# Where normalised tokens are transposed in a fused graph-network kernel: TensorE and PSUM, or VectorE blocks and DMAs

## The chip, the cores and the metric

The kernel runs on one core of a Trainium2 chip. The metric is the device time of one execution in microseconds (us), the median of several runs. Beside it stands a profiled execution, whose records (the trace) give each instruction's start and duration on TensorE, VectorE, ScalarE, GpSimd and SyncE, and each DMA's issue and landing.

## The reference

The input is x, 128 graphs of 64 nodes with 256 features, and an adjacency matrix for each graph. Two blocks are computed, each added to its input. The first is one graph-attention layer with 8 heads. The second is three layers of attention, layer norm and feed-forward network, and the change is in that one:

```
h = relu(layernorm(x))                       # input of the second block
for l in range(3):
    si, sj = x @ attn_w[l, :d], x @ attn_w[l, d:]
    scores = leaky(si[:, :, None] + sj[:, None, :] + attn_b[l])
    attn = softmax(where(mask, scores, -inf))
    agg  = einsum('bij,bjd->bid', attn, x)
    h    = layernorm(x + agg, g1[l], beta1[l])
    ff   = gelu(h @ W1[l] + b1[l]) @ W2[l] + b2[l]      # 256 -> 1024 -> 256
    x    = layernorm(h + ff, g2[l], beta2[l])
```

All is in float32. Products of the feed-forward network are made from rounded values and remainders: hi x hi, lo x hi and hi x lo.

## The kernel before

The program has two parts. The first (lines 112 to 561) runs the first block; the second (lines 563 to 1150) runs the three layers. In the second part the 8192 tokens lie in 64 tiles of 128 (two graphs each); four tiles make a group of 512 tokens, and there are 16 groups. A lap takes four groups (QG) through three layers, so 12 slots (SLOTS), and there are four laps: 48 slots. In a slot the feed-forward network of one unit U (a group in a layer) is computed, and the attention and norm of the next unit, U + 1, are prepared beside it. There is no scheduler: each engine has its own program, and the order in each function `some` is the order of the engine's instructions. Semaphores tie them: `wait_ge` on an engine, and `pause` on the queues.

What an engine does in a slot s, in order (c is one of the 8 chunks of 128 hidden features):

- TensorE: `hidden(c)`, six matmuls of 512 columns out of nT_hi and nT_lo (normalised tokens, features on partitions) into one of three PSUM banks; two chunks later `output(c)`, twelve matmuls of 256 columns out of hid_hi and hid_lo. Behind hidden(0) stands `turn_attn`, behind hidden(1) `aggregate`, behind output(0) `spread`, and behind output(3), in the step c = 5, `turn_n` of U + 1: eight transposes of 128x128 from n_tok to the two banks NT_B, which are AGG's too. `hidden(0)` waits until nT_lo is made (s_nlo).
- ScalarE: `gelu(c)` in place in PSUM, `high(c)` (hid_hi, rounded), in c = 2 and 3 `norm_y`, in c = 4 `norm_n` (n_tok of U + 1), in c = 5 `split_n` (nT_hi, rounded from NT_B), and at the end `exp` of U + 2, with a table load on either side.
- VectorE: `take_y` (feed-forward result plus base), `row_sums`, `stats_y`, `spread_y` for U - 1 and the next; `low(0)`, `low(1)` (hid_lo, the remainders); `residual` and `stats_n` of U + 1; `low(2)`, `spread_n`, `low(3)`, `scores` of U + 2, `low(4)`, `low(5)`, `split_n` (nT_lo), `low(6)`, half of `dots_of` of U + 3, `low(7)`, the other half, `diagonal`.
- GpSimd: `make_base` (n_tok times g1 plus c1, in place, for take_y), `scale_y`, `finish`, `scale_n`, `post`.
- SyncE: `exchange` of U + 2 (two DMAs that bring the other graph's half of x to x_other), `put_out` and `refill` in some slots (stores and loads of 512 KB).

The wait at the start of `hidden` and the two halves of the split read:

```
if c == 0:
    pe.wait_ge(s_nlo, KD * (U + 1))
...
act.wait_ge(s_nT, KD * V + k + 1)
act.copy(nT_hi[:, s % 2, k, :], NT_B[k][:]).then_inc(s_nhi, 1)
...
dve.tensor_tensor(nT_lo[:, s % 2, k, :], NT_B[k][:], nT_hi[:, s % 2, k, :].bitcast(F32),
                  ALU.subtract).then_inc(s_nlo, 1)
```

## Time and profile before

| | us |
|---|---|
| median of 3 runs | 1663.23 |
| lowest and highest | 1660.3, 1664.78 |
| profiled execution, its own time | 1663.78 |
| its span, first to last instruction | 1662.0 |
| TensorE busy | 1524.7 (92%) |
| VectorE busy | 1378.4 (83%) |
| ScalarE busy | 1087.1 (65%) |
| GpSimd busy | 891.4 (54%) |
| mean granted TensorE clock, share of full | 0.972 |

Busy time counts the instructions of an engine, not its waits. A busy TensorE isn't an engine at its peak, as matmuls are pipelined and overlap in the records; the distance from one start to the next tells more than a duration. The first hidden chunk of the second part starts at 385 us, so some 1275 of the 1662 us are slots. In the trace L12 is line 12 of the kernel, an arrow points from what is read to what is written, and a bracket names how long the engine had been idle and what released it. SPq is SyncE's queue; an entry there is the time that the issue of a DMA takes, not the transfer.

### The profile page before, as it was taken

The page shows a single profiled execution, that of the slowest core. Times are in us where ns is not written, and L with a number is a line of the kernel's source. Part 1 is how long each engine was busy: PE and PEld are TensorE (multiplying, and loading weights), DVE is VectorE, ACT ScalarE, POOL GpSimd, SP SyncE. Part 2 cuts the span into 40 slices and gives each one's busy share as a digit, 9 for nine tenths or more (in the row PEclk, how much of TensorE's full clock was granted, in tenths as well). Part 3 has the DMA queues.
Part 4 walks back from the last instruction along what each step waited for, and adds up shares of the span by engine and source line. Part 5 has one row for each costly group of instructions (what it writes and reads, how often), then busy time and mean ns, then how long its engine had stood idle before and what let it go on. Part 6 is the DMA issues. An engine that isn't in the chain of part 4 may idle for free. (4 is left out here: it accounts for less than half of the span.)

```text
span 1662.0 us, 37278 instructions
## 1 busy us (share of the span) xinstructions
PE 1524.7 (92%) x11360; PEld 1282.6 (77%) x11360; DVE 1378.4 (83%) x4302; ACT 1087.1 (65%) x1946; POOL 891.4 (54%) x1008
## 2 busy tenths in 40 slices
PE   6888888827999999998999999899999999999995
PEld 6566666616888888887888888788888888888885
DVE  2889999967988989887888988888898888988852
ACT  1667777714677677665767666576777766677663
POOL 1667777723455355563545456444545656355464
PEclk9999999957999999999999999999999999999998
DMA  6233333250000011110001111100011211000001
GB/s 183 81 122 120 100 113 113 77 186 18 7 14 14 13 39 47 57 62 11 7 14 29 45 49 64 34 8 14 14 39 29 80 33 39 7 14 7 14 26 51
DMA packets 70894, 83.00 MB, mean 50 GB/s; under 512 B 29264, under 2 KB 54096, under 8 KB 70736
## 3 DMA queue, kind: packets, MB, share of 16 engines
q1 hardware_dynamic: 69104, 74.76, 15.2%
q0 software_dynamic: 816, 3.15, 0.6%
q10 hardware_dynamic: 816, 3.15, 0.5%
q8 instruction: 80, 1.31, 0.3%
q14 instruction: 78, 0.64, 0.1%
HBM read 38.95 MB, written 25.17 MB: 39 GB/s over the span
## 5 line engine op out<-in xcount | busy, mean ns | idle before, releaser
L805 ACT ACTIVATE bank<-bank,b_col 128x512 f32<-128x512 f32 x384 | 253.0, 659 | 365.2 <-PE bank L753 364.9
L765 PE MATMUL bank<-w_hi,hid_hi 128*128 128x256 f32 x1536 | 443.3, 289 | 17.8 <-DVE hid_lo L965 13.0
L765 PE MATMUL bank<-w_hi,hid_lo 128*128 128x256 f32 x1536 | 433.2, 282 | 0.0
L765 PE MATMUL bank<-w_lo,hid_hi 128*128 128x256 f32 x1536 | 432.8, 282 | 0.0
L965 DVE TENSOR_TENSOR hid_lo<-bank,hid_hi 128x512 fp32r<-128x512 f32 x384 | 259.1, 685 | 146.5 <-ACT hid_hi L810 143.0
L765 PEld LDWEIGHTS bank<-w_hi,hid_hi 128*128 128x128 f32 x1536 | 289.3, 188 | 53.8 <-DVE hid_lo L965 41.5
L753 PE MATMUL bank<-nT_hi,w_hi 128*128 128x512 f32 x768 | 318.2, 414 | 6.2 <-issue 4.8
L753 PE MATMUL bank<-nT_hi,w_lo 128*128 128x512 f32 x768 | 305.0, 397 | 4.8 <-issue 4.8
L753 PE MATMUL bank<-nT_lo,w_hi 128*128 128x512 f32 x768 | 304.0, 396 | 0.0
L765 PEld LDWEIGHTS bank<-w_lo,hid_hi 128*128 128x128 f32 x1536 | 289.6, 189 | 10.3
L765 PEld LDWEIGHTS bank<-w_hi,hid_lo 128*128 128x128 f32 x1536 | 289.4, 188 | 0.0
L924 POOL TENSOR_TENSOR rs_f<-ve_f,minus_half 128x4 f32<-128x4 f32 x48 | 48.9, 1018 | 423.8 <-DVE ve_f L994 423.8
L1008 DVE CUSTOM_DVE_ANT_0 dots<-x_cur,att_row 128x256 f32<-128x256 f32 x384 | 226.8, 591 | 14.1 <-DMA adj_raw<-in_adj_dram 4.0
L810 ACT CAST hid_hi<-bank 128x512 fp32r<-128x512 f32 x384 | 226.2, 589 | 13.2
L753 PEld LDWEIGHTS bank<-nT_hi,w_hi 128*128 128x128 f32 x768 | 146.0, 190 | 47.1 <-issue 28.6
L753 PEld LDWEIGHTS bank<-nT_hi,w_lo 128*128 128x128 f32 x768 | 145.4, 189 | 34.3
L753 PEld LDWEIGHTS bank<-nT_lo,w_hi 128*128 128x128 f32 x768 | 146.3, 190 | 17.8
L917 POOL TENSOR_TENSOR rs_a<-ve_a,minus_half 128x4 f32<-128x4 f32 x48 | 48.5, 1011 | 180.1 <-DVE ve_a L1084 180.1
L907 POOL TENSOR_TENSOR n_tok<-n_tok,g_row 128x512 f32<-128x512 f32 x96 | 122.6, 1301 | 15.7 <-PE bank L743 12.5
L911 POOL TENSOR_TENSOR n_tok<-n_tok,c_row 128x512 f32<-128x512 f32 x96 | 130.6, 1385 | 0.0
L815 ACT ACTIVATE y_tok<-y_tok,nm_f,rs_f 128x256 f32<-128x256 f32 x192 | 104.9, 597 | 10.0 <-POOL nm_f L926 9.6
L832 ACT ACTIVATE n_tok<-n_tok,nm_a,rs_a 128x256 f32<-128x256 f32 x192 | 99.8, 593 | 12.3 <-POOL nm_a L919 12.3
(122 smaller groups left out, 3076.9 us busy)
## 6 DMA issues: line engine op xcount, KB each, us to landing
x_other<-x_cur SPq DMA_DIRECT2D x96, 128.0 KB, 2.4
xin<-in_x_dram SPq DMA_DIRECT2D x16, 512.0 KB
first_block_out<-x_res SPq DMA_DIRECT2D x16, 512.0 KB
second_block_in<-x_act SPq DMA_DIRECT2D x16, 512.0 KB
x_cur<-second_block_in SPq DMA_DIRECT2D x16, 512.0 KB, 3.7
x_fin<-first_block_out SPq DMA_DIRECT2D x16, 512.0 KB, 3.6
out_dram<-x_fin SPq DMA_DIRECT2D x16, 512.0 KB, 2.9
xh_other<-xh SPq DMA_DIRECT2D x128, 33.0 KB, 1.9
```

What stands on the lines that cost most here:

```text
L753: mm = pe.matmul(HID[(CF * s + c) % 3][:], w[:, l, k, c * P:(c + 1) * P], a[:, s % 2, k, :], start=(k == 0 and p == 0), stop=(k == KD - 1 ...
L765: mm = pe.matmul(FF[t // 2][:, (t % 2) * D:(t % 2 + 1) * D], a[:, r, t * P:(t + 1) * P], w[:, l, c, :], start=(c == 0 and t % 2 == 0 and p ...
L805: act.activation(h[:], h[:], ACT.Gelu, bias=b1_col[:, l, c:c + 1]).then_inc(s_gelu, 1)
L810: act.copy(hid_hi[:, (CF * s + c) % HRING, :], HID[(CF * s + c) % 3][:]).then_inc(s_hi, 1)
L815: act.activation(y_tok[:, par, t, :], y_tok[:, par, t, :], ACT.Identity, bias=nm_f[:, t:t + 1], scale=rs_f[:, t:t + 1]).then_inc(s_yn, 1)
L832: act.activation(n_tok[:, s % 2, t, :], n_tok[:, s % 2, t, :], ACT.Identity, bias=nm_a[:, t:t + 1], scale=rs_a[:, t:t + 1]).then_inc(s_n, 1)
L907: pool.tensor_tensor(base[:, h], base[:, h], g1_row[:, l].unsqueeze(1).broadcast_to([P, TG // 2, D]), ALU.mult).then_inc(s_base, 1)
L911: pool.tensor_tensor(base[:, h], base[:, h], c1_row[:, l].unsqueeze(1).broadcast_to([P, TG // 2, D]), ALU.add).then_inc(s_base, 1)
L917: pool.tensor_tensor(rs_a[:], ve_a[:], minus_half[:], ALU.pow).then_inc(s_rsa, 1)
L924: pool.tensor_tensor(rs_f[:], ve_f[:], minus_half[:], ALU.pow).then_inc(s_rsf, 1)
L965: dve.tensor_tensor(hid_lo[:, r, :], HID[(CF * s + c) % 3][:], hid_hi[:, r, :].bitcast(F32), ALU.subtract).then_inc(s_split, 1)
L1008: dve.tensor_tensor_reduce(dots[:], x_cur[:, g, t, :], att_row[:, l, j, :], 1.0, 0.0, ALU.mult, ALU.add, dst[:, t:t + 1]).then_inc(s_dots, 1)
```

## The change

The transposes on TensorE go. In their place VectorE turns n_tok in blocks of 32x32 (`turn_n`, behind low(4)) into a new buffer n_turned: within each quarter of 32 partitions, features now lie on partitions, but each quarter still holds its own tokens. SyncE then carries the 16 pairs of quarter and block to their partitions of nT_lo (`move_n`): 16 DMAs of 32 partitions with two runs of 512 bytes each. ScalarE rounds nT_hi from nT_lo, in step c = 7 instead of 5, and VectorE subtracts in place, behind low(7) instead of low(5). The columns of nT now stand in the order quarter, tile, token; `high` and `low` bring the hidden values back to the order tile, quarter, token as they write hid_hi and hid_lo (`by_block`, `by_tile`). AGG has its banks alone, and `aggregate` gets a wait for the residual of the unit before. To make room, mask_sum, dots and leaky2 share scored2's buffer, with one more wait in `dots_of`.

```diff
-            AGG = NT_B = (bank[6], bank[7])
+            AGG = (bank[6], bank[7])
+            n_turned = sb("n_turned", [P, KD, P // 32, TOK // 4], where=second)
+            mask_sum, dots = scored2, scored2[:].rearrange("p t j -> p (t j)")
...
+            def by_block(a):
+                return a.rearrange("p (q t j) -> p q t j", q=P // 32, t=TG)
+            def by_tile(a):
+                return a.rearrange("p (t q j) -> p q t j", q=P // 32, t=TG)
...
+                def move_n(V, s):
+                    pause(sp, s_turn, TG * V + TG, s_own_sp)
+                    pause(sp, s_hid, CF * (V - 1), s_own_sp)
+                    for q in range(P // 32):
+                        for b in range(P // 32):
+                            sp.dma_start(nT_lo[b * 32:(b + 1) * 32, s % 2, :, q * P:(q + 1) * P].bitcast(F32),
+                                         n_turned[q * 32:(q + 1) * 32, :, b, :]).then_inc(s_moved, 16)
...
+                    pause(pe, s_u, TG * V, s_own_pe)
...
-                def turn_n(V, s):
-                    for k in range(KD):
-                        if k == 0:
-                            pe.wait_ge(s_n, TG * (V + 1))
-                        for t in range(TG):
-                            mm = pe.transpose(NT_B[k][:, t * P:(t + 1) * P], n_tok[:, s % 2, t, k * P:(k + 1) * P], ident[:])
-                        mm.then_inc(s_nT, 1)
...
                 def split_n(V, s):
+                    act.wait_ge(s_moved, 256 * V + 256)
                     for k in range(KD):
-                        act.wait_ge(s_nT, KD * V + k + 1)
-                        act.copy(nT_hi[:, s % 2, k, :], NT_B[k][:]).then_inc(s_nhi, 1)
+                        act.copy(nT_hi[:, s % 2, k, :], nT_lo[:, s % 2, k, :].bitcast(F32)).then_inc(s_nhi, 1)
...
-                            if nxt and c == 5:
+                            if nxt and c == 7:
                                 split_n(U + 1, s + 1)
...
-                    pool.wait_ge(s_nT, KD * (V + 1))
+                    pool.wait_ge(s_turn, TG * (V + 1))
...
+                def turn_n(V, s):
+                    at_least(dve, s_moved, 256 * V)
+                    for t in range(TG):
+                        dve.wait_ge(s_n, TG * V + t + 1)
+                        dve.transpose(n_turned[:].rearrange("p k b (t j) -> p (k b) t j", t=TG)[:, :, t, :],
+                                      n_tok[:, s % 2, t, :].rearrange("p (b j) -> p b j", j=32)).then_inc(s_turn, 1)
...
                         low(U, s, 4)
+                        if nxt:
+                            turn_n(U + 1, s + 1)
                         low(U, s, 5)
-                        if nxt:
-                            split_n(U + 1, s + 1)
                         low(U, s, 6)
...
                         low(U, s, 7)
+                        if nxt:
+                            split_n(U + 1, s + 1)
```

VectorE, from hid_lo of chunk 4 in the first slot to the first dots behind it, before. L965 is hid_lo, L1089 nT_lo.

```order
L1051 TENSOR_TENSOR shifted<-leaky,top 128x256 [waits attn_ready,score_steps]
L965 TENSOR_TENSOR hid_lo<-bank,hid_hi 128x512 [waits hidden_hi] x2
L1089 TENSOR_TENSOR nT_lo<-bank_7,nT_hi 128x512 [waits nT_hi_ready] x2
L965 TENSOR_TENSOR hid_lo<-bank,hid_hi 128x512 [waits hidden_hi]
L1008 ISA dots,s_src<-x_cur,att_row 128x256 [waits dots_done,group_loaded3]
```

And now, two pieces: from the scores to chunks 5 and 6, and chunk 7 with what stands behind it.

```order
L1061 TENSOR_TENSOR shifted<-scored,top 128x256 [waits attn_ready,score_steps]
L973 TENSOR_TENSOR hid_lo<-bank,hid_hi 128x4x4x32 [waits hidden_hi]
L1101 STREAM_TRANSPOSE n_turned<-n_tok 128x8x32 [waits n_ready,nT_moved]
L1101 STREAM_TRANSPOSE n_turned<-n_tok 128x8x32 [waits n_ready] x3
L973 TENSOR_TENSOR hid_lo<-bank,hid_hi 128x4x4x32 [waits hidden_hi] x2
```

```order
L1018 ISA s_dst 128x1
L973 TENSOR_TENSOR hid_lo<-bank,hid_hi 128x4x4x32 [waits hidden_hi]
L1107 TENSOR_TENSOR nT_lo<-nT_lo,nT_hi 128x512 [waits nT_hi_ready] x2
L1018 ISA scored,s_src<-x_cur,att_row 128x256 [waits dots_done]
L1018 ISA s_src 128x1
```

The subtraction for nT_lo moved from between chunks 5 and 6 to behind chunk 7, ahead of the second half of the dots; the four block transposes came in between chunks 4 and 5.

ScalarE, from chunk 5 to the first gelu of the next slot, before:

```order
L810 CAST hid_hi<-bank 128x512 [waits ff_chunk,gelu]
L838 CAST nT_hi<-bank_7 128x512 [waits nT] x2
L805 ACTIVATE bank<-bank,b_col 128x512 [waits hidden]
L810 CAST hid_hi<-bank 128x512 [waits ff_chunk,gelu]
L805 ACTIVATE bank<-bank,b_col 128x512 [waits hidden]
L810 CAST hid_hi<-bank 128x512 [waits ff_chunk,gelu]
L821 ACT_TABLE_LOAD [waits attn_T_ready]
L821 ACTIVATE attn<-shifted 128x2x2x64 [waits shifted_ready]
```

And now, from chunk 6:

```order
L813 ACTIVATE bank<-bank,b_col 128x512 [waits hidden]
L818 CAST hid_hi<-bank 128x4x4x32 [waits ff_chunk,gelu]
L813 ACTIVATE bank<-bank,b_col 128x512 [waits hidden]
L818 CAST hid_hi<-bank 128x4x4x32 [waits ff_chunk,gelu]
L846 CAST nT_hi<-nT_lo 128x512 [waits nT_moved]
L846 CAST nT_hi<-nT_lo 128x512
L829 ACT_TABLE_LOAD [waits attn_T_ready]
L829 ACTIVATE attn<-shifted 128x2x2x64 [waits shifted_ready]
L813 ACT_TABLE_LOAD
```

The rounding of nT moved from behind chunk 5 to behind chunk 7, and stands ahead of the exponential.

SyncE's queue in a slot of the first laps, before:

```order
L29 ISA [waits aggregated]
L29 ISA [waits x_new]
L684 DMA x_other<-x_cur 64x512 [waits x_other_ready]
L685 DMA x_other<-x_cur 64x512
L29 ISA [waits aggregated]
```

And now:

```order
L29 ISA [waits aggregated]
L29 ISA [waits x_new]
L690 DMA x_other<-x_cur 64x512 [waits x_other_ready]
L691 DMA x_other<-x_cur 64x512
L29 ISA
L29 ISA [waits n_turned_in_blocks]
L699 DMA nT_lo<-n_turned 32x2x128 [waits hidden]
L699 DMA nT_lo<-n_turned 32x2x128 x15
L29 ISA [waits aggregated]
```

Two DMAs a slot became eighteen, and the 16 new ones stand behind a wait for VectorE.

## Rows read from the trace of the kernel before

**Rows 1.** The page: busy us, share of the span and instructions of each engine.

```profile
PE 1524.7 (92%) x11360; PEld 1282.6 (77%) x11360; DVE 1378.4 (83%) x4302; ACT 1087.1 (65%) x1946; POOL 891.4 (54%) x1008
```

**Rows 2.** Line 979 (min/median/max ns, first and last start), then VectorE's timeline late (start, us).

```profile
L979 DVE TENSOR_TENSOR y_tok<-bank,n_tok x192: 410/415/425, 418.3 to 1645.2; 128x256 f32<-128x256 f32 x192
```

```profile
1621.30 1.42 DVE L979 TENSOR_TENSOR y_tok<-bank,n_tok 128x256 f32<-128x256 f32 x4 [2.27 <-PE bank L765]
```

**Rows 3.** Timeline of TensorE, the eight transposes and the next matmul.

```profile
1010.13 1.04 PE L743 MATMUL bank<-ident,n_tok 128*128 128x128 f32 x8
1010.92 0.48 PE L753 MATMUL bank<-nT_hi,w_hi 128*128 128x512 f32 x1
```

**Rows 4.** Timeline of TensorE, a slot's first hidden matmul and first output matmul.

```profile
1233.55 0.39 PE L753 MATMUL bank<-nT_hi,w_hi 128*128 128x512 f32 x1
...
1239.19 0.39 PE L765 MATMUL bank<-w_hi,hid_hi 128*128 128x256 f32 x1
```

**Rows 5.** Timeline of ScalarE in the slot before and at that start.

```profile
1221.43 1.57 ACT L832 ACTIVATE n_tok<-n_tok,nm_a,rs_a 128x256 f32<-128x256 f32 x3
...
1229.79 0.59 ACT L810 CAST hid_hi<-bank 128x512 fp32r<-128x512 f32 x1
...
1232.12 1.28 ACT L805 ACT_TABLE_LOAD   x1
...
1235.72 0.38 ACT L827 COPY attn_T<-bank 128x256 f32<-128x256 f32 x1
```

**Rows 6.** Timeline of VectorE, one slot from the second half of the dots.

```profile
1206.26 0.41 DVE L1008 CUSTOM_DVE_ANT_0 dots<-x_cur,att_row 128x256 f32<-128x256 f32 x1
...
1209.08 1.41 DVE L979 TENSOR_TENSOR y_tok<-bank,n_tok 128x256 f32<-128x256 f32 x4
...
1212.83 1.28 DVE L965 TENSOR_TENSOR hid_lo<-bank,hid_hi 128x512 fp32r<-128x512 f32 x2
...
1219.72 1.32 DVE L1046 SCALAR_TENSOR_TENSOR leaky<-scored 128x256 f32<-128x256 f32 x1
...
1222.39 0.68 DVE L965 TENSOR_TENSOR hid_lo<-bank,hid_hi 128x512 fp32r<-128x512 f32 x1
...
1225.05 1.29 DVE L1089 TENSOR_TENSOR nT_lo<-bank,nT_hi 128x512 fp32r<-128x512 f32 x2 [0.16 <-ACT nT_hi L838]
```

**Rows 7.** Timeline of VectorE, the mask, in groups of the first layer only.

```profile
1021.03 0.42 DVE L1027 TENSOR_TENSOR mask_sum<-adj_raw,node_of 128x256 f32<-128x256 int32 x1
1021.49 0.29 DVE L1030 TENSOR_SCALAR mask<-mask_sum 128x256 f32<-128x256 f32 x1
```

**Rows 8.** SyncE's issues by line (ns), landings (us), a cheap issue, the page's landing.

```profile
L684 SPq DMA_DIRECT2D x_other<-x_cur x48: 461/462/493, 363.8 to 1562.3; - x48
...
L685 SPq DMA_DIRECT2D x_other<-x_cur x48: 583/590/855, 364.4 to 1562.8; - x48
...
L242 SPq DMA_DIRECT2D xh_other<-xh x64: 462/590/1576, 37.2 to 329.7; - x64
...
DMA to landing us min/median/max: 1.8/1.9/4.4
...
19.54 0.37 SPq L206 DMA_DIRECT2D xin<-in_x_dram  x1
...
x_other<-x_cur SPq DMA_DIRECT2D x96, 128.0 KB, 2.4
```

**Rows 9.** Windows: busy us of the engines, then TensorE's granted clock, DMA share, GB/s.

```profile
758.00:759.00 1.00, 0.00 (x0) 0.00 (x0) 0.53 (x2) 0.00 (x0) 0.00 (x0) 0.50 0.03 8
760.00:761.00 1.00, 0.84 (x3) 0.65 (x3) 1.00 (x4) 0.00 (x0) 0.00 (x0) 0.50 0.00 0
763.00:764.00 1.00, 1.00 (x4) 0.71 (x4) 0.46 (x1) 0.51 (x2) 0.71 (x2) 0.50 0.00 0
```

**Rows 10.** Timeline of TensorE ahead of the first slot.

```profile
381.90 1.97 PE L743 MATMUL bank<-ident,n_tok 128*128 128x128 f32 x8 [6.64 <-ACT n_tok L832]
385.27 0.79 PE L753 MATMUL bank<-nT_hi,w_hi 128*128 128x512 f32 x1 [1.40 <-DVE nT_lo L1089]
```

More of the change, by code:

```diff
@@ L570, in graph_net @@
             mask = sb("mask", [P, QG, TG, N], where=second)
-            mask_sum = sb("mask_sum", [P, TG, N], where=second)
-            dots = sb("dots", [P, D], where=second)
             s_src, s_dst = (sb(n, [P, TG], where=second) for n in ("s_src", "s_dst"))
@@ L578, in graph_net @@
             same_graph_r = sb("same_graph_r", [P, P], F32R, where=second)
-            scored2, leaky2, shifted2 = (sb(n, [P, TG, N], where=second) for n in ("scored2", "leaky2", "shifted2"))
+            scored2, shifted2 = (sb(n, [P, TG, N], where=second) for n in ("scored2", "shifted2"))
+            mask_sum, dots = scored2, scored2[:].rearrange("p t j -> p (t j)")
             top2 = sb("top2", [P, TG], where=second)
@@ L809, in high @@
                     at_least(act, s_ff, CF * U + c + 1 - HRING)
-                    act.copy(hid_hi[:, (CF * s + c) % HRING, :], HID[(CF * s + c) % 3][:]).then_inc(s_hi, 1)
+                    act.copy(by_tile(hid_hi[:, (CF * s + c) % HRING, :]), by_block(HID[(CF * s + c) % 3][:])).then_inc(s_hi, 1)
                 def norm_y(U, par, ts):
@@ L859, in some @@
                                 norm_n(U + 1, s + 1)
-                            if nxt and c == 5:
+                            if nxt and c == 7:
                                 split_n(U + 1, s + 1)
@@ L964, in low @@
                     dve.wait_ge(s_hi, CF * U + c + 1)
-                    dve.tensor_tensor(hid_lo[:, r, :], HID[(CF * s + c) % 3][:], hid_hi[:, r, :].bitcast(F32),
-                                      ALU.subtract).then_inc(s_split, 1)
+                    dve.tensor_tensor(by_tile(hid_lo[:, r, :]), by_block(HID[(CF * s + c) % 3][:]),
+                                      by_tile(hid_hi[:, r, :].bitcast(F32)), ALU.subtract).then_inc(s_split, 1)
                 def take_y(i, s):
@@ L1007, in dots_of @@
                             at_least(dve, s_dots, 8 * V + n)
-                            dve.tensor_tensor_reduce(dots[:], x_cur[:, g, t, :], att_row[:, l, j, :], 1.0, 0.0,
+                            if n == 0:
+                                at_least(dve, s_sh, V)
+                            dve.tensor_tensor_reduce(dots, x_cur[:, g, t, :], att_row[:, l, j, :], 1.0, 0.0,
                                                      ALU.mult, ALU.add, dst[:, t:t + 1]).then_inc(s_dots, 1)
@@ L1088, in split_n @@
                         dve.wait_ge(s_nhi, KD * V + k + 1)
-                        dve.tensor_tensor(nT_lo[:, s % 2, k, :], NT_B[k][:], nT_hi[:, s % 2, k, :].bitcast(F32),
-                                          ALU.subtract).then_inc(s_nlo, 1)
+                        dve.tensor_tensor(nT_lo[:, s % 2, k, :], nT_lo[:, s % 2, k, :].bitcast(F32),
+                                          nT_hi[:, s % 2, k, :].bitcast(F32), ALU.subtract).then_inc(s_nlo, 1)
                 def before():
@@ L1102, in before @@
                     spread_n(0)
+                    turn_n(0, 0)
                     scores(0, 1)
```

13 lines of the change are left out of this document (7 added, 6 removed).

## The prediction

> **What bounds the kernel now.** I read the busy shares first [rows 1]: TensorE is busy 92% of the span, VectorE 83%, the others much less. The change lies wholly in the second part, so the next view is the one that gives the length of a slot (one group of 512 tokens through one layer). VectorE takes the feed-forward result of a slot once per slot; the first of these 48 groups starts at 418.3 us, the 47th at 1621.3 [rows 2]. That is 46 periods in 1203.0 us, 26.15 us each. In the last slots, which have nothing of a later slot in them, VectorE waits 2.27 us for TensorE's result [rows 2]; in a full slot both are nearly full, and TensorE is what the 92% says it is, the bound. One slot's first hidden chunk starts on it at 1233.55 us [rows 4]. How much slack the feed of nT has is the question of this change.
>
> In the slot before that start, ScalarE ends the normalisation of n_tok at 1221.43 + 1.57 = 1223.0 us, goes on with chunks 5 to 7 and ends its rounding of chunk 7 (hid_hi) at 1230.38 [rows 5]. VectorE ends hid_lo of chunk 4 at 1222.39 + 0.68 = 1223.07 [rows 6]. Now nT_lo is ready at 1225.05 + 1.29 = 1226.3 [rows 6], 7.2 us before TensorE wants it.
>
> **The change part by part.**
>
> *Taken from TensorE.* The eight transposes hold the engine from 1010.13 to 1010.92 us, when the next matmul starts: 0.79 us a group [rows 3], 48 times 38 us. All of it is on the path, since TensorE is the bound, but only as long as it stays the bound.
>
> *Added to VectorE.* Four block transposes of 128x256 a group, behind hid_lo of chunk 4. No row shows this operation. The nearest are VectorE's other passes over 128x256 f32: four additions of a slot in 1.41 us [rows 6]. I take 1.47 us for the four. From below, the cheapest pass over 128x256 (mask, one source) takes 0.29 us [rows 7], so 1.2 for four; from above, the slowest (leaky) takes 1.32 us [rows 6], so 5.3. n_tok is ready at 1223.0, hid_lo of chunk 4 at 1223.07, so the transposes run from there to 1224.55.
>
> The Trainium skill ("VectorE: DVE Perf Modes", The three transpose paths) says that VectorE's transpose works in 32x32 blocks only, and its rules for authors send a 128x128 transpose to TensorE where PSUM will do as its goal. That speaks against the change; it gives the blocks no price that would change the sum, and no run so far shows it.
>
> *Added to SyncE.* Sixteen DMAs of 32 KB a group, one behind the other in one queue. This is where the change is decided. The queue takes 0.46 us to issue the first of a pair from SBUF to SBUF, and 0.59 for the second in both kinds of exchange [rows 8]; with the gap of 0.04 between two issues that is 0.50 to 0.63, and I take 0.57. The cheapest issue in the trace, a load from DRAM, takes 0.37, with the gap 0.41 [rows 8]. From issue to landing the exchange of 33 KB takes 1.8 to 1.9 us, the one of 128 KB 2.4 [rows 8]; I take 2.0 for the last of the 16. From the end of the turn to the landing of all: 0.1 + 15 x 0.57 + 2.0 = 10.65 us (bounds 0.1 + 15 x 0.41 + 1.8 = 8.05, and 0.1 + 15 x 0.63 + 2.4 = 11.95). In today's slot the last would land at 1224.55 + 10.65 = 1235.2. ScalarE's rounding of nT now stands behind hid_hi of chunk 7, which is done at 1230.38. So ScalarE would wait 4.8 us there, and TensorE's hidden chunk, due at 1233.55 - 0.79 = 1232.8, would wait for the rounding and VectorE's subtraction as well. The cover is gone.
>
> *What is queued behind the waits.* On ScalarE the weights of a later slot (exp between two table loads, the last of which ends at 1233.40 [rows 5], 3.0 us after hid_hi of chunk 7) and the first gelu. On VectorE, whose subtraction stands behind hid_lo of chunk 7: half of the dot products, the diagonals, the residual with the feed-forward result, its statistics, and only then hid_lo of the next slot's chunk 0. These fill the time before TensorE's start today; now they come after it. So the new period is a ring, and I add it up from the landing L of a group's last DMA to that of the next:
> - rounding and subtraction of nT: 1.08 us for ScalarE's two, 1.29 for VectorE's two, overlapping by one; ScalarE reads SBUF and not PSUM now, where a 128x256 pass takes about 0.15 us more (1.57 for three of n_tok's, 0.38 for attn_T's out of PSUM [rows 5]). L + 2.1. TensorE starts here.
> - half of the dots, and the diagonals, 1206.26 to 1209.08, 2.82 [rows 6], and the mask in the groups of the first layer (0.8, from 1021.03 to the end of 1021.49 + 0.29 [rows 7], in a third of the groups, so 0.28): L + 5.2
> - residual, sums and statistics, 1209.08 to 1212.83, 3.75: L + 8.95. hid_lo of chunk 0 starts.
> - hid_lo of chunks 0 to 3, residual and statistics of the next group, and the scores, 1212.83 to 1222.39, 9.56, then hid_lo of chunk 4, 0.68: L + 19.2. TensorE's chunk 4 and the normalisation behind it keep pace with this, as now (1223.0 and 1223.07)
> - the four transposes, 1.47: L + 20.65
> - the DMAs, 10.65: **31.3 us** a period, 5.15 more than now.
>
> TensorE needs 5.64 us from its first hidden matmul to the first output chunk (1233.55 to 1239.19 [rows 4]), so it is ready at L + 7.7 and waits until L + 9.65. From there it has at most 26.15 - 5.64 - 0.79 = 19.7 us of work, is through at L + 29.4, and stands idle for about 4 us before the next start at L + 33.4.
>
> *The clock.* Such gaps cost more than themselves. At one place in the second part TensorE sat idle for some microseconds, and the granted clock reads 0.50 (1.2 GHz instead of 2.4) at 758, and still at 760, where TensorE is busy again, and at 763 [rows 9]. So I take half the clock for the first 4 us of each slot: 2.0 us lost, TensorE ready at L + 9.7, just when VectorE is. I cost it at nothing, covered by VectorE's L + 9.65; the cover is used up to the last.
>
> *The rest.* The strided views of hid_hi and hid_lo move the same 128x512 elements, in runs of 32; I take 0.59 and 0.69 us as now. The base on GpSimd waits for the turn instead of TensorE's transposes and is 5.3 us of work with 15 us before it is read. The shared buffers (dots, mask_sum, leaky) are written in an order VectorE has anyway. The exchange of x and the loads and stores on SyncE's queue now stand behind a wait and 16 issues, but each is wanted most of a slot later. Aggregation's new wait is for a residual of the slot before. All nothing.
>
> **The sum.** Made against the profiled execution's 1663.8 us (span 1662.0), which stands 0.5 above the median of 1663.23. 47 slots start behind such a landing: 47 x 5.15 = 242. Before the first slot the transposes start at 381.90 and the first hidden chunk at 385.27, 3.4 us [rows 10]; now 0.4 + 10.65 + 2.1 = 13.2, so 10 more, and 1 for the last slot. 1663.8 + 242 + 11 = 1917.
>
> **The rivals.**
> *Cheaper issues.* The sixteen differ only in addresses, and could be issued at the price of the cheapest row. At 0.41 to 0.47 each and a landing of 1.8, the period is 28.7 to 29.6, the time 1795 to 1840. Against it: every pair from SBUF to SBUF has the 0.59 in it.
>
> *The clock breaks through.* If the half clock lasts over all of TensorE's 5.64 us of early work, it is ready at L + 13.4, 3.7 us behind VectorE: up to 47 x 3.7 = 174 more, 1990 to 2090. For it: six microseconds at half clock around 760 [rows 9]. Against it: two of them lay in idle time.
>
> *The transfer is hidden (faster).* If all 16 land before TensorE would be short of nT, only the 0.79 us remains: 1663.8 - 38 = 1626. For that L must be 1232.8 - 2.1 = 1230.7, which leaves 6.1 us after the turn; less 0.1 and 2.0, 15 issues in 4.0 us, 0.27 each. With 0.32 each the gain is eaten and the time stands still. Both are under the 0.37 of the cheapest row, so this needs a queue faster than any here.
> The Trainium skill ("DMA: Bandwidth & Descriptors", Issuing engines are not separate DMA queues) calls the sequencer's time for a DMA usually small relative to the DMA itself; by that rule it is this rival that comes out. The rows disagree: 0.46 to 0.59 us of issue against 1.8 to 2.4 to landing, and there are sixteen.
>
> **How the numbers follow.** A measurement of this kernel can tell about 0.3% from no change. Forecast, 1840 to 1990, centre 1917: 0.71. Cheaper issues, 1795 to 1840: 0.13. Clock, 1990 to 2090: 0.10. Hidden and faster: 0.05. Within 0.3%: 0.01. The range 1800 to 1995 leaves out nearly all of the clock's case and the hidden one, under 2 in 10; its top is a period of 33.0 us, which takes in issues of 0.63 with a landing of 2.4 (32.6) and dearer transposes up to 0.47 us each, not the 1.32. Faster 0.05, same 0.01, slower 0.94.
>
> **What would show it.** Slots 31 us apart by the residual's row; 16 issues of 0.46 to 0.59 us in SyncE's queue behind each turn; ScalarE and VectorE idle before the rounding and the subtraction of nT, released by the DMA; TensorE idle some 5 us before each slot's first hidden chunk, and again 2 us before the first output chunk, released by hid_lo; a granted clock under 1.00 in every slot; transposes of about 0.4 us. I am wrong if the issues pipeline to under 0.37 us, if VectorE's string after the subtraction is shorter than its rows today, or if the block transpose costs a microsecond each.

## The result, and the profile after

The changed kernel takes **1991.17 us** (median of 4 runs, 1990.8 to 1992.43) against 1663.3 for the kernel before: ratio 1.1975, 95% interval 1.1955 to 1.1996. The profiled execution took 1992.43 us, its span is 1990.6, TensorE's mean granted clock 0.910 where it had been 0.972. The forecast was 1917, in a range of 1800 to 1995: slower as forecast, 74 us above the centre and just under the top.

The page of the changed kernel, with the rows that answer to [rows 1] and [rows 8]; the two groups are the first hidden matmuls and ScalarE's rounding of nT, where the last column is the idle time before them and its releaser:

```profile
PE 1583.1 (80%) x10976; PEld 1313.1 (66%) x10976; DVE 1462.6 (73%) x4494; ACT 1088.9 (55%) x1946; POOL 893.9 (45%) x1008
...
L764 PE MATMUL bank<-nT_hi,w_hi 128*128 128x512 f32 x768 | 357.6, 466 | 261.7 <-DVE nT_lo L1107 261.7
...
L846 ACT CAST nT_hi<-nT_lo 128x512 fp32r<-128x512 f32 x96 | 54.6, 615 | 339.1 <-DMA nT_lo<-n_turned 339.1
```

TensorE fell from 92% to 80% of the span, and VectorE from 83% to 73%: no engine bounds the kernel now. TensorE lost 384 instructions (48 x 8 transposes) and yet is busy 58 us longer, since much of it runs at half clock. ScalarE waits 339 us for the moved blocks: a ring of waits sets the time, that is, a chain of operations in which each engine waits for the next and the last for the first of the slot before.

The lines of the new operations in the changed kernel: durations min/median/max in ns, then first and last start in us, and the landings.

```profile
L699 SPq DMA_DIRECT2D nT_lo<-n_turned x768: 585/597/1858, 383.4 to 1944.0; - x192
...
DMA to landing us min/median/max: 1.8/1.9/3.3
...
L1101 DVE STREAM_TRANSPOSE n_turned<-n_tok x192: 393/398/446, 381.4 to 1933.5; 128x256 f32<-128x256 f32 x192
...
L846 ACT CAST nT_hi<-nT_lo x96: 612/616/618, 395.4 to 1946.4; 128x512 fp32r<-128x512 f32 x96
```

Line 846 gives the period: two roundings a group, so the last group's first starts about 0.5 us before 1946.4, and (1945.9 - 395.4) / 47 = **32.99 us** a slot, where it had been 26.15 [rows 2].

One slot of the changed kernel on the timelines of ScalarE, TensorE, VectorE and SyncE (start, us, what, and in brackets the idle time before it and its releaser), with a later start for the next landing:

```profile
1326.40 1.14 ACT L846 CAST nT_hi<-nT_lo 128x512 fp32r<-128x512 f32 x2 [6.52 <-DMA nT_lo<-n_turned]
...
1327.05 1.29 DVE L1107 TENSOR_TENSOR nT_lo<-nT_lo,nT_hi 128x512 fp32r<-128x512 f32 x2 [4.97 <-ACT nT_hi L846]
...
1328.48 0.79 PE L764 MATMUL bank<-nT_hi,w_hi 128*128 128x512 f32 x1 [4.65 <-DVE nT_lo L1107]
...
1331.08 1.41 DVE L987 TENSOR_TENSOR y_tok<-bank,n_tok 128x256 f32<-128x256 f32 x4
...
1334.84 0.69 DVE L973 TENSOR_TENSOR hid_lo<-bank,hid_hi 128x512 fp32r<-128x512 f32 x1
1335.81 0.69 DVE L973 TENSOR_TENSOR hid_lo<-bank,hid_hi 128x512 fp32r<-128x512 f32 x1 [0.29 <-ACT hid_hi L818]
...
1341.51 0.69 DVE L973 TENSOR_TENSOR hid_lo<-bank,hid_hi 128x512 fp32r<-128x512 f32 x1 [0.97 <-ACT hid_hi L818]
...
1346.08 1.41 DVE L1101 STREAM_TRANSPOSE n_turned<-n_tok 128x256 f32<-128x256 f32 x4
...
1347.72 10.76 SPq L699 DMA_DIRECT2D nT_lo<-n_turned  x16
...
1359.81 1.14 ACT L846 CAST nT_hi<-nT_lo 128x512 fp32r<-128x512 f32 x2 [7.04 <-DMA nT_lo<-n_turned]
```

From one rounding to the next the ring closes: rounding, VectorE's string to hid_lo of chunk 0, on to the transposes, then 12.3 us in which SyncE's queue sends sixteen blocks and the last one lands. ScalarE sits idle for the last 7.0 us of these. Against the forecast, piece by piece (the means are over all the slots that the trace shows whole):

| piece of the ring | forecast | this slot | mean |
|---|---|---|---|
| landing to hid_lo of chunk 0 | 8.95 | 8.44 | 8.8 |
| to the first transpose | 10.24 | 11.24 | 10.6 |
| four transposes | 1.47 | 1.41 | 1.43 |
| end of the turn to the next landing | 10.65 | 12.32 | 12.2 |
| period | 31.3 | 33.41 | 33.0 |

The moves are the piece that is off: 1.5 of the 1.7 us a slot. ScalarE's and VectorE's passes over the strided views take what they took before (588 against 589 ns for hid_hi, 683 against 685 for hid_lo), so these cost nothing.

### The profile page after: what moved, and what is told of

It reads as the page before. It is cut to its first block and busy times, and to the rows that moved or that the text cites. A ratio compares the mean times of both kernels' runs of the same rounds, so it can differ in the third digit from the quotient of the medians.

```text
span 1990.6 us, 37733 instructions
## 1 busy us (share of the span) xinstructions
PE 1583.1 (80%) x10976; PEld 1313.1 (66%) x10976; DVE 1462.6 (73%) x4494; ACT 1088.9 (55%) x1946; POOL 893.9 (45%) x1008
## 3 DMA queue, kind: packets, MB, share of 16 engines
q8 instruction: 78, 1.28, 0.3%
## 5 line engine op out<-in xcount | busy, mean ns | idle before, releaser
L764 PE MATMUL bank<-nT_hi,w_hi 128*128 128x512 f32 x768 | 357.6, 466 | 261.7 <-DVE nT_lo L1107 261.7
L764 PEld LDWEIGHTS bank<-nT_hi,w_hi 128*128 128x128 f32 x768 | 166.8, 217 | 310.2 <-issue 211.0
L764 PE MATMUL bank<-nT_lo,w_hi 128*128 128x512 f32 x768 | 336.5, 438 | 0.0
L764 PE MATMUL bank<-nT_hi,w_lo 128*128 128x512 f32 x768 | 334.5, 435 | 0.0
L1018 DVE CUSTOM_DVE_ANT_0 scored<-x_cur,att_row 128x256 f32<-128x256 f32 x384 | 250.1, 651 | 14.5 <-DMA adj_raw<-in_adj_dram 4.2
L1107 DVE TENSOR_TENSOR nT_lo<-nT_lo,nT_hi 128x512 fp32r<-128x512 f32 x96 | 62.1, 688 | 266.8 <-ACT nT_hi L846 266.8
L846 ACT CAST nT_hi<-nT_lo 128x512 fp32r<-128x512 f32 x96 | 54.6, 615 | 339.1 <-DMA nT_lo<-n_turned 339.1
L764 PEld LDWEIGHTS bank<-nT_hi,w_lo 128*128 128x128 f32 x768 | 165.4, 215 | 41.6
L764 PEld LDWEIGHTS bank<-nT_lo,w_hi 128*128 128x128 f32 x768 | 167.1, 218 | 21.5
```

What stands on the lines that cost most here:

```text
L764: mm = pe.matmul(HID[(CF * s + c) % 3][:], w[:, l, k, c * P:(c + 1) * P], a[:, s % 2, k, :], start=(k == 0 and p == 0), stop=(k == KD - 1 ...
L846: act.copy(nT_hi[:, s % 2, k, :], nT_lo[:, s % 2, k, :].bitcast(F32)).then_inc(s_nhi, 1)
L1018: dve.tensor_tensor_reduce(dots, x_cur[:, g, t, :], att_row[:, l, j, :], 1.0, 0.0, ALU.mult, ALU.add, dst[:, t:t + 1]).then_inc(s_dots, 1)
L1107: dve.tensor_tensor(nT_lo[:, s % 2, k, :], nT_lo[:, s % 2, k, :].bitcast(F32), nT_hi[:, s % 2, k, :].bitcast(F32), ALU.subtract).then_inc( ...
```

## The experiments

Two theories stood at the start. **The train**: the sixteen issues, one behind the other in one queue, are the price, and all else is small. **The clock and the ring**: TensorE's idle time brings the half clock, and that, or the place of the subtraction on VectorE, carries much of it. A third question was whether TensorE's transposes had been worth anything.

### Four wide moves in place of sixteen

```diff
 for q in range(P // 32):
-    for b in range(P // 32):
-        sp.dma_start(nT_lo[b*32:(b+1)*32, s % 2, :, q*P:(q+1)*P], n_turned[q*32:(q+1)*32, :, b, :])
+    sp.dma_start(nT_lo[:, s % 2, :, q*P:(q+1)*P], n_turned[:, :, q, :])
...                                      # the waits count 4 landings, not 16
```

> The 16 DMAs of 32 partitions become 4 of 128 partitions, each with the quarter q of every partition: the same 512 KB a group, in the same buffer, but not to the partitions where they belong, so the features of the tokens are mixed up between partitions. If the serial issue in SyncE's queue is the cause (16 issues took 10.76 us in the changed kernel), the moves take about 0.2 + 3 x 0.65 + 2.3 = 4.5 us instead of 12.3, the landing comes before ScalarE is through with chunk 7, the wait is gone and TensorE binds again: 1640 us (1625 to 1670). If the bytes or their shape (128 or 32 partitions at once) are the cause, the time stays above 1900.

Measured: 1704.3 us, ratio 1.0242 [1.0216, 1.0268], clock 0.971. The same bytes in a quarter of the issues give back 287 of the 328 us, 6.1 us a slot. The blocks stay on their partitions, so what TensorE multiplies is not the right data, but the work is the same. SyncE's timeline and its line in this kernel, and TensorE's wait for hid_lo between 500 and 1650 us (total, times, longest):

```profile
1225.93 2.64 SPq L698 DMA_DIRECT2D nT_lo<-n_turned  x4
...
L698 SPq DMA_DIRECT2D nT_lo<-n_turned x192: 608/622/1556, 385.6 to 1655.6; - x192
...
PE bank L775 <- DVE hid_lo L972: 82.1, 82, 2.1
```

An issue of 128 KB costs what one of 32 KB does (622 and 597 ns), so the price goes by the count: 2.64 us instead of 10.76. ScalarE's wait for the moves shrinks from 339.1 us in 48 waits to 13.3 in 13: the transfer is nearly hidden. This run alone doesn't separate the count from the shape of a move (128 partitions at once instead of 32) or from its crossing partitions; the runs with two queues and by way of DRAM do. But the time was 34 us above the top of what was expected. 41 us over the kernel before stay with the train gone, and TensorE no longer has its transposes. TensorE waits for hid_lo instead, and the next two runs show for which of its chunks.

### The place alone, without turn or moves

The kernel before, with its rounding and subtraction of nT moved to chunk 7, where the change has them:

```diff
-if nxt and c == 5:
+if nxt and c == 7:
     split_n(U + 1, s + 1)                # ScalarE
...
     low(7)
+    if nxt: split_n(U + 1, s + 1)        # VectorE, was behind low(5)
```

> The kernel before, with its transposes on TensorE, but with the rounding and the subtraction of nT in the place that the change gives them (behind chunk 7 on both engines). If the late place alone costs, VectorE's string behind it comes 1.3 us later and TensorE waits for hid_lo of chunk 0: up to 1.3 us a slot, 1664 to 1725, I take 1690. If the place is free, and all of the loss is the moves, 1664 within 3 us.

Measured: 1720.71 us, 1.0347 [1.032, 1.0373], clock 0.971: +57 us, 1.2 us a slot. VectorE's timeline and TensorE's there, and TensorE's wait for hid_lo between 450 and 1650 us:

```profile
1218.55 1.28 DVE L1089 TENSOR_TENSOR nT_lo<-bank,nT_hi 128x512 fp32r<-128x512 f32 x2
...
1227.06 0.39 PE L765 MATMUL bank<-w_hi,hid_hi 128*128 128x256 f32 x1 [1.04 <-DVE hid_lo L965]
...
PE bank L765 <- DVE hid_lo L965: 56.9, 50, 1.9
```

The subtraction now stands ahead of VectorE's 6.6 us of dots, diagonals, residual and statistics, and hid_lo of chunk 0 comes later by its 1.28 us. TensorE feels nearly all of it: its matmuls wait 56.9 us for hid_lo (50 waits) between 450 and 1650 us, where the kernel before has 10.1 (20). By the brackets of TensorE's timeline over the whole run, 57.3 us (43 waits) stand in front of output(0), which needs hid_lo of chunk 0. So VectorE's string behind chunk 7 had almost no slack before the change: 1.28 us more on it cost 1.2. It rarely held TensorE up there (9.2 us in 13 such waits), so this doesn't say that a shorter string would gain anything.

### Six of the eight transposes left out

```diff
 def turn_n(V, s):                        # TensorE, kernel before
-    for t in range(TG):
+    for t in range(1):
```

> The kernel before with 2 of its 8 TensorE transposes a group (the first tile of either half); the other tiles are left out, so nT holds other data there. If TensorE's transposes are on the path, 0.59 us a slot goes: 1636 us (1630 to 1645). If the ring of before runs through VectorE alone, as the 56 us for a place 1.28 us later on VectorE suggest, it stays at 1664.

Measured: 1648.78 us, 0.9911 [0.9896, 0.9926]: 15 us, where 28 would be the full price of 48 x 0.59. By proportion the eight transposes are worth some 20 us (an estimate, 15 x 8/6). TensorE's wait for hid_lo between 450 and 1650 us, then VectorE's and TensorE's timelines:

```profile
PE bank L765 <- DVE hid_lo L965: 37.3, 57, 0.7
```

```profile
1216.16 1.37 DVE L1008 CUSTOM_DVE_ANT_0 dots<-x_cur,att_row 128x256 f32<-128x256 f32 x1
...
1217.58 1.39 DVE L1008 CUSTOM_DVE_ANT_0 dots<-x_cur,att_row 128x256 f32<-128x256 f32 x1
...
1220.57 0.38 PE L765 MATMUL bank<-w_hi,hid_hi 128*128 128x256 f32 x1 [0.65 <-DVE hid_lo L965]
```

Waits for hid_lo take part of what TensorE is given (37.3 us in 57 waits, 10.1 in 20 before), but it is another chunk than in the run on the place: 28.9 us (44 waits) are for hid_lo of chunk 7, which had 1.6 (8) in the kernel before. VectorE comes late to it because the dots ahead of it are longer. They now come earlier against GpSimd's work on the base (the first takes 1.37 us here and 0.81 in a slot of the kernel before), and over all 384 dots the mean rises from 591 to 654 ns, 24 us; the last experiment shows the same effect. So this run says nothing on the string behind chunk 7.

Both kinds of wait are in the kernel with four wide moves: 55.0 us (44) for chunk 0 and 33.0 (44) for chunk 7, with a mean of 655 ns for a dot. That is 88 us where the kernel before had 11; less the 38 us of transposes, 39, near the 41 that are left (an estimate from sums of waits).

### The train split over two queues

SyncE issues ten of the sixteen, ScalarE three behind its chunk 5 and three behind chunk 6:

```diff
-for n in range(16):                      # SyncE
+for n in range(10):
...
+if nxt and c in (5, 6):                  # ScalarE
+    move_part(U + 1, s + 1, range(3*c - 5, 3*c - 2))
```

> The changed kernel with 10 of a group's 16 DMAs issued by SyncE and 6 by ScalarE's queue, three behind its rounding of chunk 5 and three behind chunk 6, where it has 1.2 and 1.5 us of idle time. If the issues in one queue are what the ring waits for, six of them at 0.666 us leave it: 4.0 us a slot less, 1803 us (1740 to 1830; lower if TensorE's gap gets too short for the half clock). If the DMA engines or the partitions set the pace, whichever queue issues, it stays above 1950.

Measured: 1793.32 us, 1.0782 [1.0766, 1.0799], clock 0.971: 198 us back, near the 1803 that was expected. SyncE and ScalarE in this kernel:

```profile
1254.12 7.57 SPq L699 DMA_DIRECT2D nT_lo<-n_turned  x10
...
1253.92 1.90 ACTq L847 DMA_DIRECT2D nT_lo<-n_turned  x3
1256.64 2.18 ACTq L847 DMA_DIRECT2D nT_lo<-n_turned  x3
...
1262.98 1.14 ACT L853 CAST nT_hi<-nT_lo 128x512 fp32r<-128x512 f32 x2 [2.77 <-DMA nT_lo<-n_turned]
```

Both queues issue at the same time, at 0.63 to 0.76 us each. In the mean SyncE's ten take 0.69 each, 6.89 us in all where sixteen had taken 10.63, so the two queues slow each other little. The period between roundings shrinks by 4.1 us, 3.7 of it from the turn to the landing and 0.4 from the subtraction to the transposes; the mean clock is back at 0.971, though not every slot starts at full clock (this one reads 0.50 at 1266). The Trainium skill ("DMA: Bandwidth & Descriptors", Issuing engines are not separate DMA queues) says that initiating on several engines saves only the sequencer's time, usually small. What it saves is indeed that time alone; it is 198 us here and not small, since sixteen issues stand in a row on the path.

### The same traffic without anything that waits for it

```diff
+def ride(V, s):                          # SyncE, kernel before, once a group
+    pause(sp, s_n, TG * V + TG, s_own_sp)
+    for q in range(4):
+        for b in range(4):
+            sp.dma_start(aside[b*32:(b+1)*32, q*P:(q+1)*P], w2_hi[q*32:(q+1)*32, 0, b, 0:P])
...                                      # aside is a buffer that nobody reads
```

> The kernel before, with 16 DMAs a group added in SyncE's queue at the place of the moves (behind the normalised tokens), each of 32 partitions with one run of 512 bytes from the weights to a buffer nobody reads: all that SyncE and the DMA engines do for the moves (half the bytes), with nobody waiting. If the queue and the traffic cost nothing by themselves and only the wait for the landing does, 1664 within 5. If they get in the way of the exchange, the loads or the engines, 1680 or more.

Measured: 1664.32 us, 1.0004 [0.9995, 1.0014]. Sixteen small moves a group, and the exchange of x behind them in the queue, cost nothing when no engine waits for them. Its moves carry half the bytes of the change's, so this excludes a cost of the queue, not every cost of traffic.

### By way of DRAM

```diff
-for q in range(4):
-    for b in range(4):
-        sp.dma_start(nT_lo[b*32:(b+1)*32, ...], n_turned[q*32:(q+1)*32, :, b, :])
+sp.dma_start(turn_d[s % 2], n_turned)    # wait for it, then
+for b in range(4):
+    sp.dma_start(nT_lo[b*32:(b+1)*32, ...], turn_d[s % 2] as (q f)(k b t) -> f k q b t, [b])
```

> The changed kernel with the 16 moves replaced by one store of n_turned to DRAM (512 KB, whole partitions), a wait for it, and four loads of 32 partitions each that pick their blocks from DRAM. Five issues and two landings instead of sixteen issues and one: 0.2 + 0.5 + 2.6 + 4 x 0.65 + 2.3, about 8.2 us instead of 12.1, so 3.9 a slot less: 1808 us (1780 to 1850), although every byte goes twice and farther. If bytes or landings weigh more than issues, above 1900.

Measured: 1785.21 us, 1.0727 [1.07, 1.0755], clock 0.970. SyncE and ScalarE in this kernel:

```profile
1224.42 0.32 SPq L700 DMA_DIRECT2D turned<-n_turned  x1
1227.15 2.58 SPq L703 DMA_DIRECT2D nT_lo<-turned  x4
...
1232.31 1.14 ACT L850 CAST nT_hi<-nT_lo 128x512 fp32r<-128x512 f32 x2 [3.04 <-DMA nT_lo<-turned]
```

Twice over the memory and with a wait between, 7.9 us from the store's issue to the rounding, and still 4.2 us shorter than the 12.1 of the direct way (1347.72 to 1359.81): five issues against sixteen. In the mean over all slots the difference is 3.9 us from the turn to the landing. This is the strongest evidence for the count, since here the path is longer and the bytes are twice as many.

### The turn across the quarters by VectorE itself

No DMA at all; each of the 16 blocks of 32 partitions is turned straight to its place:

```diff
-dve.transpose(n_turned[...all partitions...], n_tok[:, s % 2, t, :])          # 4 a group
+dve.transpose(n_turned[b*32:(b+1)*32, :, q, :], n_tok[q*32:(q+1)*32, ...])    # 16 a group
```

> The changed kernel without the moves: VectorE's transposes write straight into the other quarter of the partitions, 16 instructions of 32 partitions by 256 for each group instead of 4 of 128 partitions, and the rounding waits for them alone. By the 0.40 us of one of the four, the sixteen hold VectorE for 5.6 us instead of 1.4, partly in the 2.4 us where it waits for hid_hi now. No landing is in the ring: 28.3 us a slot, 1765 us (1720 to 1850). If a transpose into other partitions costs more, above 1900.

Measured: 1957.67 us, 1.1761 [1.1738, 1.1784], clock 0.918. Expectation and result are 190 us apart, and the reason is in the rows: the page's line of engines, TensorE's wait for hid_lo between 500 and 1900 us (total, times, longest), the line of the transposes, and VectorE's timeline.

```profile
PE 1584.8 (81%) x10976; PEld 1322.3 (68%) x10976; DVE 1776.3 (91%) x5070; ACT 1092.0 (56%) x1946; POOL 907.1 (46%) x1008
...
PE bank L773 <- DVE hid_lo L970: 226.1, 123, 3.0
...
L1100 DVE STREAM_TRANSPOSE n_turned<-n_tok x768: 432/436/442, 383.8 to 1908.3; 32x256 f32<-32x256 f32 x192
...
1326.97 7.24 DVE L1100 STREAM_TRANSPOSE n_turned<-n_tok 32x256 f32<-32x256 f32 x16
1334.24 1.29 DVE L970 TENSOR_TENSOR hid_lo<-bank,hid_hi 128x512 fp32r<-128x512 f32 x2
```

A block transpose over 32 partitions takes 436 ns, one over 128 took 398: a quarter of the partitions doesn't make it shorter. Sixteen take 7.24 us, five times what the four took (1.41). VectorE is 91% busy and is the bound, and hid_lo of chunk 5, right behind the sixteen, comes late: TensorE's matmuls wait 226 us for hid_lo, against 40 in the changed kernel.

### The clock kept up

18 matmuls whose result nobody reads fill TensorE's wait before a group's first hidden chunk:

```diff
 # TensorE, changed kernel, after a group's last output chunk
+if nxt:
+    pause(pe, s_u, TG * (U + 2), s_own_pe)
+    for n in range(18):
+        pe.matmul(AGG[0][:], w1_hi[:, 0, 0, 0:P], nT_hi[:, s % 2, 0, :], ...)
```

> The changed kernel with 18 matmuls of 512 columns added on TensorE behind the last output chunk of a slot, about 4.2 us of its 5.2 us of idle time; they write a bank that nobody reads. If the half clock at the start of a slot (6 us at 0.50) delays the ring, as the two waits of hid_lo for hid_hi (0.29 and 0.97 us) say, the granted clock stays at 1.00 and the time falls by about 1.2 us a slot, to 1935 (1920 to 1955). If the low clock is covered by VectorE's string, as the prediction had it, the time stays at 1991 within 5 us, with the clock up all the same.

Measured: 1981.15 us, 1.1906 [1.1877, 1.1935], clock 0.974: between the two cases that were expected. What the clock did in the changed kernel, by windows (the columns of [rows 9]: busy engines, then granted clock, DMA share, GB/s):

```profile
1327.00:1328.00 1.00, 0.00 (x0) 0.00 (x0) 0.95 (x2) 0.98 (x3) 0.00 (x0) 0.87 0.84 195
1328.00:1329.00 1.00, 0.52 (x1) 0.50 (x2) 0.96 (x4) 0.99 (x2) 0.00 (x0) 0.50 0.01 2
1333.00:1334.00 1.00, 1.00 (x4) 0.57 (x2) 1.00 (x4) 0.00 (x0) 0.00 (x0) 0.50 0.00 0
1334.00:1335.00 1.00, 1.00 (x13) 0.54 (x16) 0.90 (x9) 0.57 (x1) 0.00 (x0) 0.71 0.00 0
```

TensorE begins its slot at half clock (0.50, 1.2 GHz) and keeps it for six microseconds of work. With the matmuls in between the clock holds (0.974 in the mean), and yet only 10 us come back, 0.2 a slot. The half clock is nearly all covered by VectorE's string: it reached the ring only in the waits of 0.29 and 0.97 us for hid_hi in the slot above. By the means, the way from the subtraction to the transposes becomes 0.4 us shorter and the moves take 0.2 more. What covers it shows in TensorE's wait for hid_lo between 500 and 1900 us:

```profile
PE bank L776 <- DVE hid_lo L977: 81.0, 85, 3.8
```

That is 40.3 us in 51 waits in the changed kernel. The new ones are for chunk 0 (53.4 us in 45 waits over the run, 9.9 in 9 before): with the clock up, TensorE is ready earlier and stands waiting for VectorE.

### The subtraction later on VectorE

First right before hid_lo of the next group's chunk 0, and the weights' exp ahead of the rounding on ScalarE:

```diff
     low(7)
-    if nxt: split_n(U + 1, s + 1)        # VectorE
     ...dots, diagonal, residual, statistics...
+    split_n(U, s)                        # next turn, before low(0)
...                                      # and ScalarE's exp ahead of its split_n
```

> The changed kernel with VectorE's subtraction for nT_lo moved behind the dots, diagonals, residual and statistics (5.9 us of work), ahead of hid_lo of chunk 0, and on ScalarE the exponential ahead of the rounding of nT: what was queued behind the waits now runs in the idle time. If VectorE's string behind the landing is part of the ring, hid_lo of chunk 0 comes when TensorE's first chunk is ready, and TensorE's own path at half clock takes over: about 17.9 instead of 19.0 us from its first hidden chunk to the end of the turn, 1.1 a slot less, 1940 us (1915 to 1965). If only the DMAs and the clock set the period, it stays at 1991.

Measured: 2045.44 us, 1.2296 [1.2266, 1.2327], clock 0.899: slower by 54 us where 50 less was expected. ScalarE and VectorE in this kernel:

```profile
1353.72 1.14 ACT L846 CAST nT_hi<-nT_lo 128x512 fp32r<-128x512 f32 x2 [4.81 <-DMA nT_lo<-n_turned]
...
1355.86 1.29 DVE L1107 TENSOR_TENSOR nT_lo<-nT_lo,nT_hi 128x512 fp32r<-128x512 f32 x2
```

The first rounding is done at 1354.3, but VectorE is in the middle of what I had put ahead, and comes 1.5 us late. TensorE then starts 3.6 us after the landing instead of 2.1, from a longer idle time. I had asked what fills VectorE's wait and not whether it is longer than the wait. So the second try puts only the dots and diagonals (2.8 us) ahead; the exp stays ahead of the rounding on ScalarE, as in the first:

```diff
     low(7)
-    if nxt: split_n(U + 1, s + 1)        # VectorE
     dots_of(i, s + 3, range(2, 4)); diagonal(...)
+    if nxt: split_n(U + 1, s + 1)
```

> As late, but only the dots and diagonals (2.8 us, done before the landing) go ahead of VectorE's subtraction; residual and statistics stay behind it. In late the subtraction itself came 1.5 us after its operand, because 7 us of work stood ahead of it. If that is why late lost, TensorE starts 2.1 us after the landing again, hid_lo of chunk 0 no longer waits for VectorE, and a slot is 0.9 us shorter than in the changed kernel: 1948 us (1930 to 1970). If moving VectorE's string is harmful for another reason, 1991 or more.

Measured: 1971.9 us, 1.1855 [1.1837, 1.1873]: 19 us back, 2 short of the expected range. The same with the 18 matmuls added:

> late2 and warm together: the dots and diagonals ahead of VectorE's subtraction, and 18 added matmuls in TensorE's gap. Alone they gave 19 and 10 us. If VectorE's string covers the half clock in the changed kernel and the clock covers the string in late2 (two ways through the ring of nearly the same length), both together give more than the sum: about 2 us more a slot than late2, 1875 us (1860 to 1905). If the two do not hide each other, 1991 - 29 = 1962.

Measured: 1883.9 us, 1.1312 [1.1293, 1.1331], clock 0.975: 107 us back, where the two alone gave 10 and 19. The waits of three kernels, over 500 to 1850 or 1900 us (in total, times, longest), first the changed kernel, then the later subtraction, then both:

```profile
DVE hid_lo L973 <- ACT hid_hi L818: 97.2, 76, 1.8
...
PE bank L776 <- DVE hid_lo L973: 40.3, 51, 3.0
```

```profile
DVE hid_lo L973 <- ACT hid_hi L818: 203.4, 162, 2.2
```

```profile
DVE hid_lo L977 <- ACT hid_hi L822: 142.7, 132, 2.1
```

In the changed kernel VectorE's string and TensorE's slow start run side by side and end nearly together. Shorten the string, and VectorE waits 203 us for chunks that a half-clocked TensorE hands over late; keep the clock, and TensorE waits for the string. Only both together show what either was worth.

### The dots spread, on the kernel before

If VectorE's string behind chunk 7 holds TensorE up, one of its two tiles of dots moved ahead should help:

```diff
+if nxt3: dots_of(i, s + 3, range(0, 1))     # before low(6)
 low(6)
-dots_of(i, s + 3, range(0, 2))
+dots_of(i, s + 3, range(1, 3))
 low(7)
-dots_of(i, s + 3, range(2, 4))
+dots_of(i, s + 3, range(3, 4))
```

> The kernel before, with the dot products of a slot spread otherwise on VectorE: one tile's ahead of hid_lo of chunk 6, where VectorE sits idle for 1.25 us, two behind it, and only one behind chunk 7 instead of two. The same work in another order. If VectorE's string behind chunk 7 is on the path, as place7 says, 0.94 us of it goes, up to the idle time that TensorE has in a slot: 1625 us (1610 to 1645). If it is not, 1664 within 3.

Measured: 1676.88 us, 1.0076 [1.0063, 1.009]: 13 us slower. VectorE and GpSimd in this kernel, GpSimd's second instruction also by itself:

```profile
1207.52 1.49 DVE L1008 CUSTOM_DVE_ANT_0 dots<-x_cur,att_row 128x256 f32<-128x256 f32 x1
1209.05 1.39 DVE L1008 CUSTOM_DVE_ANT_0 dots<-x_cur,att_row 128x256 f32<-128x256 f32 x1
...
1213.80 0.41 DVE L1008 CUSTOM_DVE_ANT_0 dots<-x_cur,att_row 128x256 f32<-128x256 f32 x1
...
1206.18 2.54 POOL L907 TENSOR_TENSOR n_tok<-n_tok,g_row 128x512 f32<-128x512 f32 x2 [0.24 <-PE bank L743]
...
1207.44 1.28 POOL L907 TENSOR_TENSOR n_tok<-n_tok,g_row 128x512 f32<-128x512 f32 x1
...
1208.68 2.91 POOL L911 TENSOR_TENSOR n_tok<-n_tok,c_row 128x512 f32<-128x512 f32 x2
```

A dot product of two operands in SBUF takes 0.41 us with GpSimd idle and 1.4 to 1.5 while GpSimd makes the base, with two operands of its own (1206.18 to 1211.6). The times look like a wait of one GpSimd instruction and not like a slower pass: GpSimd's second starts at 1207.44, just before the dot of 1207.52, and the third at 1208.68; that dot ends at 1209.01, 0.33 us later. Moving the tile earlier moved it under GpSimd's work: over all 384 the mean rises from 591 to 730 ns, 54 us of VectorE's time. TensorE's waits for hid_lo of chunk 0 are gone altogether, but the kernel before had only 9.2 us of them to give, and 35.1 us (44 waits) for chunk 7 came in their place.

## Why the prediction came out as it did

The sign and the ring that sets the time were right; the centre was 74 us low. The range held narrowly, 4 us under its top: the moves went past their own upper bound (12.2 against 11.95 us), and the rest of the ring came near its centre.

- **What bounds the kernel.** Partly wrong. I took TensorE alone as the bound. The place alone (+57) shows that VectorE's string behind chunk 7 had almost no slack, and the left-out transposes (15 of 28 us) that its dots ahead of chunk 7 had little. The forecast did not suffer, because its sum went along VectorE's string. What suffered is the rival of the hidden transfer: it was priced at 1626, TensorE's 38 us, and with the train nearly gone the time was 1704.
- **Taken from TensorE, 38 us.** Too much even where it counts: six of eight gave 15 us and not 28, some 20 for all by the estimate above. In the changed kernel it counts for nothing, as TensorE is not the bound.
- **The four transposes, 1.47 us.** 1.41 in the slot shown, 1.43 in the mean, bounds 1.2 to 5.3: right, near the lower end.
- **The sixteen issues, 0.57 each.** This is the term that was mis-sized. SyncE's timeline has sixteen in 10.76 us, 0.67 each from start to start, 0.66 in the mean over all slots, above my top bound of 0.63. I had taken the middle of 0.50, the first of a pair, and 0.63, the second [rows 8]. In a train of sixteen the median issue is 597 ns, 0.63 with the gap, so all are like the second, and some take longer (up to 1858 ns), which makes the mean 0.66. With the landing (1.9 against 2.0) and 0.23 us to the first issue, the moves take 12.2 us instead of 10.65: 1.5 us x 47 = 73 us, about the size of the miss. The other 0.2 us a slot and some 4 at the first slot are made up behind the last landing, which no run took apart. What makes some of the issues longer was not found.
- **The place behind chunk 7, ScalarE's wait of 4.8 us.** Confirmed in kind: 7.0 us in the slot shown, and 339 us over the run.
- **The ring, 31.3 us.** 33.0. Its first piece was forecast 0.15 too long, its second 0.35 too short; VectorE's waits for hid_hi in it were not in the sum.
- **The clock, costed at nothing, "used up to the last".** Nearly right. The half clock lasts over the first 6 us of TensorE's work in a slot and not the first 4 us; it reaches the ring with 0.4 us a slot, and 10 us in all is what its removal gives back (the run with 18 matmuls). That lies between my nothing and the rival's 73 to 173 us more. But the cover is thin: with a shorter string the same clock is worth 88 us (1971.9 to 1883.9). The wait of 2 us before each first output chunk, named as a sign, did not come (9.9 us in 9 waits over the run): TensorE's slow start fills that time.
- **Traffic and strided views, nothing.** Right for the queue, by the run that rides along, and for the strided views, by the passes' durations. GpSimd's base comes later against VectorE's dots than I had it: the mean dot takes 651 ns instead of 591. Here VectorE then waits for the landing all the same; with four wide moves it does not, and there it costs.
- **The first slot, +10 us.** The first residual starts 14.2 us later (432.5 against 418.3 [rows 2]), some 4 more than forecast. The turn and the moves take 13.95 us there (381.4 to 395.4) and not 11.05, and the first hidden chunk runs at half clock.
- **The rivals.** Cheaper issues: no, 0.66 and not 0.41 to 0.47. The clock breaks through: the six microseconds at 0.50 are there, their price is not. Hidden: the issues are not cheap enough; and where four wide moves did hide the transfer, the gain was not there (1704 against 1626).

Where the 328 us are, by the runs: 287 are the train of sixteen against four, with the half clock inside them. The other 41 are waits for VectorE, behind the place (+57 by itself) and behind dots that GpSimd stretches, less what TensorE saves on its transposes (some 20, an estimate). How these share the 41 was not separated.

## What to carry to other kernels

Count the DMAs of a move before its bytes: in one queue each of them cost 0.6 to 0.7 us here, with 32 KB or with 128, and fewer and wider ones, a second queue, or even a round through DRAM beat sixteen direct ones. When an engine is given time back and the gain is not all there, look for which operand it waits for, and not only for which engine. When two strings run side by side in a ring and end within half a microsecond of each other, shortening one shows little; try both together before you call a cause small. Before an operation is moved, look at which engine works beside its new place, and whether what it is put ahead of can wait that long.

## What the runs showed of the hardware

- From SBUF to SBUF, 32 KB and 128 KB cost the same issue time (597 and 622 ns, median) on SyncE; a train of sixteen takes 0.66 us each where pairs had taken 0.50 to 0.63. On ScalarE's queue, three take 1.90 to 2.18 us.
- Sixteen direct moves between partitions took 12.1 us from first issue to use, one store to DRAM and four loads of it 7.9.
- VectorE's block transpose of 256 f32 elements a partition takes 398 ns over 128 partitions and 436 over 32, also where source and target lie in different quarters.
- A VectorE operation with two operands in SBUF takes 1.4 to 1.5 us instead of 0.41 while GpSimd works on two of its own. The Trainium skill ("GPSIMD Engine Reference", Specifications) says that GpSimd's interface to SBUF is shared with VectorE, and names two SBUF inputs as the case of contention. The trace agrees: the dot costs 3.4 to 3.6 times as much, and its end, 0.33 us behind that of the GpSimd instruction it met, looks like a wait for that instruction to end. So a change on a third engine can lengthen VectorE's work: with six transposes fewer on TensorE the mean dot goes from 591 ns to 654.
- Both cases of the clock stand side by side: after 4.65 us without a matmul TensorE's slot begins at 0.50, and with 18 idle-time matmuls the mean clock goes from 0.910 to 0.974. That is worth 10 us where VectorE covers it and 88 where it doesn't.
